# Norm coefficients in six GpSimd steps with one power, silu(z) by tile, z copied ahead of x's exponential, decays in one buffer

## What is computed

```python
x = x + layernorm(attn(layernorm(x)))
x = x + layernorm(ffn(layernorm(x)))

# attn(hidden)
h = rmsnorm(hidden, w_norm_in)
z, x, B, C, dt_raw = split(h @ w_in_proj)        # 256, 256, 512, 512, 8
x = silu(causal_conv4(x) + conv_b)
dt = mean_over_head_dim(softplus(dt_raw @ w_dt + b_dt))   # 8 heads of 32
y = ssd_scan(x, dt, B, C, A_log) + x * D         # state of 64 per head
y = rmsnorm(y * silu(z), w_norm_out)
return hidden + y @ w_out_proj
# ffn(input): 8 experts, the best 2 of each token, 128 -> 256 -> 128
```

## Time and profile before

| | us |
|---|---|
| median of 3 runs | 1142.01 (1137.75 to 1142.52) |
| the profiled execution | 1139.66 |
| its span in the profile | 1137.9 |
| PE busy | 1036.1 (91%) |
| DVE busy | 936.5 (82%) |
| ACT busy | 653.9 (57%) |
| POOL busy | 612.8 (54%) |

### The profile page before, as it was taken

The page is one execution under the profiler, slowest core; times in us unless marked ns, Lnnn a source line. Parts: engine busy times, 40 slices in busy tenths (PEclk is TensorE's granted clock), DMA queues, the critical chain, the costliest instruction groups (busy, mean ns, idle before and its releaser), DMA issues.

```text
span 1137.9 us, 29655 instructions
## 1 busy us (share of the span) xinstructions
PE 1036.1 (91%) x9060; PEld 869.2 (76%) x9060; DVE 936.5 (82%) x2590; ACT 653.9 (57%) x1237; POOL 612.8 (54%) x873
## 2 busy tenths in 40 slices
PE   3899998998998998988999877999999999999996
PEld 2677776776776776776778666898988888888885
DVE  5668895886786787787778766999999999999997
ACT  4778776775876776675787432444444444444442
POOL 7345563554555555455554542555555555555654
PEclk9999998998998998998999988999999999999998
DMA  6000000000000000000000300000000000000000
GB/s 181 4 3 4 3 4 5 1 4 5 3 2 5 3 2 4 4 3 3 4 3 3 97 1 1 10 11 10 9 9 9 9 9 9 9 9 9 10 11 18
DMA packets 19586, 14.41 MB, mean 13 GB/s; under 512 B 4361, under 2 KB 16929, under 8 KB 19489
## 3 DMA queue, kind: packets, MB, share of 16 engines
q1 hardware_dynamic: 19488, 13.02, 4.2%
HBM read 7.77 MB, written 4.19 MB: 11 GB/s over the span
## 4 chain that ended last, share of the span: by engine, by line
PE 55%; DVE 11%; issue 11%; POOL 10%; ACT 7%; DMA 2%; SPq 1%; POOLq 1%; DVEq 1%; ACTq 0%
PE bank L1591 16%; PE bank L1564 4%; PE bank L1565 4%; PE bank L768 4%; PE bank L1566 4%; PE bank L840 2%; PE bank L752 2%; PE bank L560 2%; DVE moe_acc L1640 2%; PE bank L562 2%; DVE moe_h L1442 2%; PE bank L561 2%; PE bank L754 2%; POOL ln_scale L497 2%; PE bank L550 2%
## 5 line engine op out<-in xcount | busy, mean ns | idle before, releaser
L1575 ACT ACTIVATE moe_hid<-bank,moe_b 128x512 f32<-128x512 f32 x256 | 167.2, 688 | 172.6 <-PE bank L1566 172.2
L1591 PEld LDWEIGHTS bank<-moe_w,moe_hid 128*128 128x128 f32 x2048 | 249.5, 193 | 21.4 <-ACT moe_hid L1575 5.8
L1591 PE MATMUL bank<-moe_w,moe_hid 128*128 128x128 f32 x2048 | 252.4, 277 | 5.3 <-DVE moe_acc L1640 2.7
L1640 DVE SCALAR_TENSOR_TENSOR moe_acc<-bank,moe_scores,moe_acc 128x128 f32<-128x128 f32 x448 | 125.6, 341 | 22.3 <-PE bank L1591 20.1
L852 ACT ACTIVATE m<-bank 128x512 f32<-128x512 f32 x128 | 70.1, 595 | 88.9 <-PE bank L754 88.9
L932 DVE TENSOR_TENSOR mg<-bank,m 128x512 f32<-128x512 f32 x128 | 82.4, 685 | 43.2 <-PE bank L768 42.7
L560 PE MATMUL bank<-thi,whi 128*128 128x512 f32 x224 | 105.9, 473 | 10.1 <-ACT bt L601 3.8
L1564 PE MATMUL bank<-moe_t_hi,moe_w_hi 128*128 128x512 f32 x256 | 113.9, 445 | 0.0
L1617 POOL TENSOR_TENSOR moe_b_mix<-moe_b_mix 128x512 f32<-128x512 f32 x80 | 107.5, 1344 | 10.2
L923 POOL TENSOR_TENSOR y<-y,zt 128x256 f32<-128x256 f32 x64 | 46.8, 731 | 118.5 <-DVE y L947 117.9
L1565 PE MATMUL bank<-moe_t_lo,moe_w_hi 128*128 128x512 f32 x256 | 102.9, 402 | 0.0
(11 more groups left out here) (178 smaller groups left out, 2530.8 us busy)
## 6 DMA issues: line engine op xcount, KB each, us to landing
out_dram<-moe_outb SPq DMA_DIRECT2D x16, 256.0 KB, 2.3
parts<-csplit SPq DMA_DIRECT2D x128, 4.0 KB
rows<-csplit SPq DMA_DIRECT2D x128, 4.0 KB
moe_w<-in_L_ffn_W_dram SPq DMA_DIRECT2D x1, 1024.0 KB, 5.5
m<-in_L_attn_w_in_proj_dram SPq DMA_DIRECT2D x1, 772.0 KB
...
```

The lines of the kernel that those rows point to most:

```text
L1575: SE.activation(hid[:, e % 2, n, :], up_banks[k % 4][:], ACT.Relu, bias=b1[:, k:k + 1]).then_inc(hid_ready.sem, 1)
L1591: mm = PE.matmul(bank[:, col(i)], hid[:, e % 2, n, col(i)], w2[:, e, n, :], start=n == 0, stop=n == FB - 1, skip_group_check=True)
L1640: DVE.scalar_tensor_tensor(out=acc[:, par, i, :], in0=y, scalar=s, in1=acc[:, par, i, :], op0=ALU.mult, op1=ALU.add).then_inc(acc_step.sem, 1)
```

## The change

- `pool_norm` has six steps. The variance gives at once var(1 + e) + ce and var + c (c the layernorm's, e the rmsnorm's epsilon), and the mean its negative, in three instructions without a wait between them. One power of 8 columns (a constant `neghalf2` twice as wide) gives both scales. A product gives the bias, a copy writes `s1`.
- `pool_silu_z` and its place in tile 0 are gone. `pool_gate` first multiplies the tile's own 256 columns of `zt` and `zsig`, waits for that product, and then gates as before.
- `zsig` has two buffers by the parity of the group. The second is the second half of `m`. ACT's first exponential of z waits for the last tile of group f - 2.
- `act_decays` has one buffer `m` and waits for the scores and x weights of tile t - 1.
- ACT's exponential of x in tile 2 stands behind the copies of z.
- SP no longer waits for silu(z) of the last group before it loads the experts' weights.
- `neghalf` is the first half of the wider constant wherever else it is used.

```diff
@@ -132,7 +132,8 @@
     ident = keep("ident", [P, P])
     ones = keep("ones", [P, P])
     zeros = keep("zeros", [P, 1])
-    neghalf = keep("neghalf", [P, TG])
+    neghalf2 = keep("neghalf", [P, 2 * TG])
+    neghalf = neghalf2[:, 0:TG]
     rank = keep("rank", [P, TG, NE])
     ident16 = keep("ident16", [P, P], BF16)
     later = keep("later", [P, P], BF16)
...
@@ -148,7 +149,7 @@
     edec = keep("edec", [P, 2, DI + NH])
     m_flat = keep("m", [P, 2 * NH * P])
     mg_flat = keep("mg", [P, 2 * NH * P])
-    m = m_flat[:].rearrange("p (b h l) -> p b h l", b=2, h=NH)
+    m = m_flat[:, 0:NH * P].rearrange("p (h l) -> p h l", h=NH)
     mg = mg_flat[:].rearrange("p (b h l) -> p b h l", b=2, h=NH)
     btok = keep("btok", [P, 2, NP * P])
     xtok = keep("xtok", [P, 2, DI])
...
@@ -187,7 +188,7 @@
     cs = sb("cs", [P, P])
     csplit = sb("csplit", [P, 2, PARTS, P], F32R)
     xraw = sb("xraw", [P, 2, NB, KC - 1 + GT])
-    zsig = sb("zsig", [P, NB, GT])
+    zsig = [sb("zsig0", [P, NB, GT]), m_flat[:, NH * P:].rearrange("p (n l) -> p n l", n=NB)]
 
 
     wraw, wf = m_flat[:, 0:PROJ], mg_flat[:, 0:WCOLS]
...
@@ -217,7 +218,7 @@
     cleared = sig("buffers_cleared", 1)
 
     ln_stats = sig("ln_stats_ready", 2 * TG)
-    coef_step = sig("ln1_coefficient_steps", 9)
+    coef_step = sig("ln1_coefficient_steps", 6)
     h_ready = sig("h_ready", TG)
     fr_done = sig("front_products_done", 16)
     thi_ready = sig("thi_ready")
...
@@ -350,7 +351,7 @@
     CONST_IDENT = 3
 
     def pool_identity(pl):
-        PL.memset(neghalf[:], -0.5).then_inc(const_step.sem, 1)
+        PL.memset(neghalf2[:], -0.5).then_inc(const_step.sem, 1)
         PL.memset(ident[:], 0.0).then_inc(const_step.sem, 1)
         pl.wait_ge(const_step.sem, 2)
         PL.affine_select(out=ident[:], in_=ident[:], compare_op=ALU.not_equal, fill=1.0, base=0,
...
@@ -491,31 +492,18 @@
         if due(f - 1):
             pl.wait_ge(h_ready.sem, h_ready.of(f - 1))
         apart(pl, f)
-        PL.tensor_scalar(lnt[:, 0, :], var, LN_EPS, None, ALU.add).then_inc(coef_step.sem, 1)
-        pl.wait_ge(coef_step.sem, coef_step.of(f, 1))
-        apart(pl, f)
-        PL.tensor_tensor(rs, lnt[:, 0, :], neghalf[:], ALU.pow).then_inc(coef_step.sem, 1)
+        PL.tensor_scalar(lnt[:, 2, :], var, 1.0 + RMS_EPS, LN_EPS * RMS_EPS, ALU.mult, ALU.add
+                         ).then_inc(coef_step.sem, 1)
+        PL.tensor_scalar(lnt[:, 3, :], var, LN_EPS, None, ALU.add).then_inc(coef_step.sem, 1)
+        PL.tensor_scalar(lnt[:, 5, :], mean, -1.0, None, ALU.mult).then_inc(coef_step.sem, 1)
         pl.wait_ge(coef_step.sem, coef_step.of(f, 2))
         apart(pl, f)
-        PL.tensor_tensor(lnt[:, 1, :], rs, rs, ALU.mult).then_inc(coef_step.sem, 1)
-        pl.wait_ge(coef_step.sem, coef_step.of(f, 3))
-        apart(pl, f)
-        PL.tensor_tensor(lnt[:, 2, :], lnt[:, 1, :], var, ALU.mult).then_inc(coef_step.sem, 1)
+        PL.tensor_tensor(lnt[:, 0:2, :].rearrange("p k t -> p (k t)"), lnt[:, 2:4, :].rearrange("p k t -> p (k t)"),
+                         neghalf2[:], ALU.pow).then_inc(coef_step.sem, 1)
         pl.wait_ge(coef_step.sem, coef_step.of(f, 4))
         apart(pl, f)
-        PL.tensor_scalar(lnt[:, 3, :], lnt[:, 2, :], RMS_EPS, None, ALU.add).then_inc(coef_step.sem, 1)
-        pl.wait_ge(coef_step.sem, coef_step.of(f, 5))
-        apart(pl, f)
-        PL.tensor_tensor(lnt[:, 4, :], lnt[:, 3, :], neghalf[:], ALU.pow).then_inc(coef_step.sem, 1)
-        pl.wait_ge(coef_step.sem, coef_step.of(f, 6))
-        apart(pl, f)
-        PL.tensor_tensor(lnt[:, 0, :], lnt[:, 4, :], rs, ALU.mult).then_inc(coef_step.sem, 1)
-        pl.wait_ge(coef_step.sem, coef_step.of(f, 7))
-        apart(pl, f)
-        PL.tensor_scalar(lnt[:, 5, :], mean, -1.0, None, ALU.mult).then_inc(coef_step.sem, 1)
-        pl.wait_ge(coef_step.sem, coef_step.of(f, 8))
-        apart(pl, f)
-        PL.tensor_tensor(lnt[:, 1, :], lnt[:, 5, :], lnt[:, 0, :], ALU.mult).then_inc(coef_step.sem, 1)
+        PL.tensor_tensor(lnt[:, 4, :], lnt[:, 5, :], lnt[:, 0, :], ALU.mult).then_inc(coef_step.sem, 1)
+        PL.tensor_copy(rs, lnt[:, 1, :]).then_inc(coef_step.sem, 1)
 
     def act_h(act, f, par, dyn):
         act.wait_ge(coef_step.sem, coef_step.of(f))
...
@@ -524,7 +512,7 @@
             act.wait_ge(fr_done.sem, fr_done.of(f - 2, 1))
         for i in range(TG):
             x = xall[:, dyn(f * TG + i, 1), :].rearrange("p o d -> p (o d)")
-            SE.activation(h[:, par, i, :], x, ACT.Identity, scale=lnt[:, 0, i:i + 1], bias=lnt[:, 1, i:i + 1]
+            SE.activation(h[:, par, i, :], x, ACT.Identity, scale=lnt[:, 0, i:i + 1], bias=lnt[:, 4, i:i + 1]
                           ).then_inc(h_ready.sem, 1)
 
 
...
@@ -637,15 +625,15 @@
         if step == 0:
             act.wait_ge(z_ready.sem, z_ready.of(f))
 
-            if due(f - 1):
-                act.wait_ge(zt_ready.sem, zt_ready.of(f - 1))
-            SE.activation(zsig[:], zt[par][:], ACT.Exp, scale=-1.0).then_inc(zsig_step.sem, 1)
+            if due(f - 2):
+                act.wait_ge(zt_ready.sem, zt_ready.of((f - 2) * TG + TG - 1))
+            SE.activation(zsig[par][:], zt[par][:], ACT.Exp, scale=-1.0).then_inc(zsig_step.sem, 1)
         if step == 1:
             act.wait_ge(zheld.sem, zheld.of(f))
-            SE.activation(zsig[:], zsig[:], ACT.Ln, bias=1.0).then_inc(zsig_step.sem, 1)
+            SE.activation(zsig[par][:], zsig[par][:], ACT.Ln, bias=1.0).then_inc(zsig_step.sem, 1)
         if step == 2:
             act.wait_ge(zsig_step.sem, zsig_step.of(f, 2))
-            SE.activation(zsig[:], zsig[:], ACT.Exp, scale=-1.0).then_inc(zsig_step.sem, 1)
+            SE.activation(zsig[par][:], zsig[par][:], ACT.Exp, scale=-1.0).then_inc(zsig_step.sem, 1)
 
     def dve_conv(dve, f, par, steps):
 
...
@@ -715,15 +703,10 @@
         if key == "zheld":
 
             dve.wait_ge(zsig_step.sem, zsig_step.of(f, 1))
-            DVE.tensor_scalar(zsig[:], zsig[:], EXP_MAX, None, ALU.min).then_inc(zheld.sem, 1)
+            DVE.tensor_scalar(zsig[par][:], zsig[par][:], EXP_MAX, None, ALU.min).then_inc(zheld.sem, 1)
         if key == "xt":
             dve.wait_ge(xsig_step.sem, xsig_step.of(f))
             DVE.tensor_tensor(xt[par][:], xraw[:, par, :, 0:GT], xt[par][:], ALU.mult).then_inc(xt_ready.sem, 1)
-
-    def pool_silu_z(pl, g, par):
-        pl.wait_ge(zsig_step.sem, zsig_step.of(g))
-        apart(pl, g)
-        PL.tensor_tensor(zt[par][:], zsig[:], zt[par][:], ALU.mult).then_inc(zt_ready.sem, 1)
 
     def pool_history(pl, f, par, first_of_batch):
 
...
@@ -845,11 +828,11 @@
     def act_decays(act, t, tp):
         for hf in range(2):
             act.wait_ge(dd_done.sem, dd_done.of(t, hf + 1))
-            if hf == 0 and due(t - 2):
-
-                act.wait_ge(mg_ready.sem, mg_ready.of(t - 2))
-                act.wait_ge(xw_ready.sem, xw_ready.of(t - 2))
-            SE.activation(m[:, tp, hf * HH:(hf + 1) * HH, :], banks[2 + hf][:].rearrange("p (h l) -> p h l", l=P),
+            if hf == 0 and due(t - 1):
+
+                act.wait_ge(mg_ready.sem, mg_ready.of(t - 1))
+                act.wait_ge(xw_ready.sem, xw_ready.of(t - 1))
+            SE.activation(m[:, hf * HH:(hf + 1) * HH, :], banks[2 + hf][:].rearrange("p (h l) -> p h l", l=P),
                           ACT.Exp).then_inc(m_ready.sem, 1)
 
     def act_turned(act, t, i, tp, fr):
...
@@ -902,7 +885,7 @@
             apart(pl, t)
             PL.tensor_tensor(xw[:, tp, :].rearrange("p (h d) -> p h d", d=HD)[:, hf::2, :],
                              xtok[:, tp, :].rearrange("p (h d) -> p h d", d=HD)[:, hf::2, :],
-                             m[:, tp, hf * HH:(hf + 1) * HH, P - 1:P].to_broadcast([P, HH, HD]),
+                             m[:, hf * HH:(hf + 1) * HH, P - 1:P].to_broadcast([P, HH, HD]),
                              ALU.mult).then_inc(xw_ready.sem, 1)
         pl.wait_ge(e_ready.sem, e_ready.of(t))
         if due(t - 1):
...
@@ -915,7 +898,11 @@
 
     def pool_gate(pl, t, i, g, par, tp):
         if i == 0:
-            pl.wait_ge(zt_ready.sem, zt_ready.of(g))
+            pl.wait_ge(zsig_step.sem, zsig_step.of(g))
+        apart(pl, t)
+        PL.tensor_tensor(zt[par][:, :, col(i)], zsig[par][:, :, col(i)], zt[par][:, :, col(i)], ALU.mult
+                         ).then_inc(zt_ready.sem, 1)
+        pl.wait_ge(zt_ready.sem, zt_ready.of(t))
         pl.wait_ge(y_step.sem, y_step.of(t))
         if due(t - 2):
             pl.wait_ge(oo_done.sem, oo_done.of(t - 2))
...
@@ -930,7 +917,7 @@
             dve.wait_ge(gg_done.sem, gg_done.of(t))
             dve.wait_ge(m_ready.sem, m_ready.of(t, hf + 1))
             DVE.tensor_tensor(mg[:, tp, heads, :], banks[4 + hf][:].rearrange("p (h l) -> p h l", l=P),
-                              m[:, tp, heads, :], ALU.mult).then_inc(mg_ready.sem, 1)
+                              m[:, heads, :], ALU.mult).then_inc(mg_ready.sem, 1)
 
     def dve_y(dve, t, i, par, tp):
```

(14 more changed lines are left out.)

## The result

The changed kernel takes 1122.28 us (median of four runs, 1120.72 to 1124.04), the kernel before beside it 1142.09: ratio 0.9835, 95% interval 0.9805 to 0.9866. Another set of runs on one chip gave 1121.43 against 1139.73, ratio 0.9848 [0.9823, 0.9874]. The forecast was 1121, range 1112 to 1132. The profiled execution took 1123.76 us, its span is 1121.9.

A forecast was written before the change was run, and what follows sets the result against it. PE, busy 91% of the span, was taken as the bound. Gains of 13.8 (loop), 1.0 (first two groups), 0.4 (group without a norm), 3.6 (start) and 0.4 (experts) sum to 19.2 us, forecast 1121, range 1112 to 1132.

The forecast's parts named there:

- The bound and the chain: Attention loop: PE bounds, busy 91%; norm, gate, square, z copies form one chain that holds PE once per group.
- Norm coefficients: POOL's norm in tile 1: six steps take 4.7 us, with 1.88 for the power of 8 columns; nine took 6.57.
- held sum of 5.4 us: Tile 1's six norm steps on POOL if DVE's two-SBUF-input instructions hold them all: 5.4 us.
- The sum per group: PE's three waits per loop group total 1.26 us; 1.15 is won, bounds 0.5 to 1.5; twelve groups 13.8.
- silu(z) by tile: POOL's gating: tile 0 loses PE's 0.34 us wait; tile 1's uncovered multiply costs 0.9 us, more if held.
- Rival 4: Tile 1: the new multiply holds DVE, which becomes the bound through y; the change does not pay, 1137 us; chance 0.09.
- Decays in one buffer: ACT's decays: the new wait for the tile before is always fulfilled, so the single buffer costs nothing.
- Start: Kernel start, where coefficients are waited for openly: 3.6 us sooner, bounds 2.0 and 4.5.
- Groups 0 and 1: First two groups, same norm but shorter waits: 0.5 us each, 1.0 in all.
- group 14: Group without a norm: 0.4 us gained from tile 0.
- The change to the experts: Passage to the experts: SyncE's wait for the last silu before the weight load goes, 0.4 us.
- Total: Whole kernel: 19.2 us gained from the profiled 1139.66, giving 1120.5, put at 1121 us.

The follow-up runs named there:

- extra_power: The changed kernel with one more power of 4 columns, never read, in tile 1's norm, not in the prologue: 1126.99 us, ratio to before 0.9895.
- silu_only: The kernel before with silu(z) multiplied by tile and the buffers it needs, nine-step norm and old order kept: 1147.87 us, ratio 1.0098.
- norm_only: The kernel before with only the norm cut to six steps: 1120.33 us, ratio 0.985.
- moved: The changed kernel with tile 1's silu multiply behind tile 0's gate and the RMS scale copy behind tile 1's gate: 1117.97 us, ratio to before 0.982.
- zt_moved: The changed kernel with only tile 1's silu multiply moved behind tile 0's gate: 1123.07 us, ratio to before 0.9852.
- buffers_only: The kernel before with only the buffers changed, decays in one and zsig in two: 1140.63 us, ratio 1.002.
- start_norm: The kernel before with the short norm in the first two groups alone: 1138.8 us, ratio 0.9994.

## Why the prediction was right, point by point

**The bound and the chain.** Right, with the chain's price too low for the norm (below). extra_power and silu_only show the chain: a gate 0.82 and 0.98 us later costs 0.87 and 0.97 us from tile 1 to 2, and PE's wait for x grows with it.

**Norm coefficients.** I took 1.88 us for the power of 8 columns; it takes 1.66 (1.73 and 1.68 at the start), 0.6 above the one of 4. The three steps take 0.6 each, near the 0.65 taken. The norm takes 4.5 us for 4.7, and the gate comes at 6.0 for 5.9. The held sum of 5.4 us, which the sentence on the Trainium skill called the right one, was not reached: the three steps were held, the product behind the power was not (0.20 us), and no gap stood ahead of the power.

**The sum per group.** The total was right, 1.15 for 1.154 (1.41 in the second profile), but its division by parts was not. I gave the z order the 0.67 us of L550 and the norm, through the gate, the 0.25 of L560. Measured, the norm alone gives 1.35, the order alone 0.76, and with the norm there the order gives 0.1 to 0.35. The step that failed is that I added the waits as if each had one cause: the wait for z is also the late gate's, for the copies stand on ACT behind the square of the gated tile. That 12.9 of the 13.85 us are idle time of PE is what the forecast rested on, and it held.

**silu(z) by tile.** Tile 0 was right: 0.42 to 0.50 us for 0.34 forecast, `dtv`'s wait gone, and L998 down from a mean of 847 to 372 ns in the loop. The cost in tile 1 was seen, 0.9 us plus hold, but netted against the norm, so the text never asked what the part does alone: it loses 0.68 us there when the norm is short and 0.97 when it is long. In this kernel no gain of it is shown: without it the ratio is 0.9823 [0.9795, 0.9852], with it 0.9835 and 0.9848. It also takes DVE's busy time in twelve groups from 372.0 to 344.6 us in silu_only, 27 us of a busy engine, for a kernel that is 9 us slower.

**Rival 4** was in part true. After's tile 1 is DVE's. In norm_only the conv's half, the halving copy behind it and the residual read

```profile
284.35 2.56 DVE L661 SCALAR_TENSOR_TENSOR xt<-xraw,cw,xt 128x512 f32<-128x512 f32 x3
286.94 0.69 DVE L652 TENSOR_SCALAR xt<-xt 128x1024 f32<-128x1024 f32 x1
...
288.86 1.33 DVE L973 SCALAR_TENSOR_TENSOR ob<-xall,ln_scale,og 128x128 f32<-128x128 f32 x4
```

and in after

```profile
281.69 2.55 DVE L661 SCALAR_TENSOR_TENSOR xt<-xraw,cw,xt 128x512 f32<-128x512 f32 x3
284.28 1.11 DVE L652 TENSOR_SCALAR xt<-xt 128x1024 f32<-128x1024 f32 x1
...
286.63 2.01 DVE L972 SCALAR_TENSOR_TENSOR ob<-xall,ln_scale,og 128x128 f32<-128x128 f32 x4
```

1.1 us more on DVE, and y of tile 2 starts at 289.65 without idling. The Trainium skill, SBUF — State Buffer, section Who interferes with whom, says that a DVE instruction with two SBUF inputs or in a two-port mode and a GpSimd instruction that reads SBUF exclude each other, the later one waiting for the whole of the earlier. The rows agree (in both kernels the first 256-column multiply of POOL beside the conv takes 1.24 us where 0.73 is usual, and the conv's three take 2.55 where they took 2.08). That the 0.68 us of the column 1 to 2 are these 1.1 us less DVE's slack there was not tried by itself; moved and zt_moved, which take the multiply out of the tile, bring them back.

**Decays in one buffer** cost nothing in the loop, as argued: ACT's decays wait for PE alone, in after 55.0 us in 39 waits. That buffers_only came out 0.2% above before stays open.

**Start** was mis-sized: 3.6 taken, 3.26 in one profile, but start_norm allows at most 2.8 and has 0.7 as its middle. The bounds of 2.0 and 4.5 left out that the landing of the weights moves by 2 us. The first h came at 8.77 us for 8.8 and the second waited 0.30 us for 2.69, but the conv ended at 26.19 us for the forecast's 25. **Groups 0 and 1** gave 0.43 for 1.0, **group 14** 0.07 for 0.4. **The change to the experts** was to give 0.4; the first profile of after has 0.8 us less of gain at its end (16.0, by the spans) than at the last tile's decay (16.8), the second 0.1 less (18.4, 18.5). Neither shows the 0.4. Group 15, for which the forecast has no term, lost too: the gain falls by 1.91 us at its start in the first profile. One of SyncE's row copies took long to issue, and PE waited for it:

```profile
606.99 1.43 SPq L1251 DMA_DIRECT2D rows<-csplit  x1
```
```profile
610.97 0.49 PE L735 MATMUL bank<-rows,parts 128*128 128x512 f32 x1 [1.58 <-DMA rows<-csplit]
```

But before has such a wait at the same place (1.21 us, behind an issue of 1.06), so this is 0.4 of the 1.91 us. Behind it the granted clock is 0.50 from 612 to 614 us, where before keeps 1.00 through the same tile (628 to 632). A long issue is in before too, at 388.62 us (1.52 us), so I take that part for chance.

**Total.** The forecast gain of 19.2 us stands against 19.8 and 18.3 by the medians of the two sets, and 16.0 and 18.4 by the spans of the two profiles. The loop has given 13.8 and 16.9 of it, for 13.8 forecast. The times agree better than the terms: start, groups 0 and 1, group 14 and the change to the experts were all put too high, and in the second profile the loop's excess of 3 us makes up for that. The 1142.01 from which the forecast counted is of three executions; the larger sets put before 2 to 3 us lower.
